# Opening of a fused cross-attention and routed-FFN kernel: scales in four chains, small loads on ScalarE's queue, weights in pieces

## The reference, cut to what matters

```python
x  = x + tanh(g_xattn) * xattn(ctx_1024, layernorm(x), ln_m_g, ln_m_b, ln_l_g, ln_l_b, Wq, Wkv, Wout)
x  = x + tanh(g_ffn)   * ffn(layernorm(x), gate_w, w1, b1, w2, b2)

def xattn(ctx, latents, ...):          # 32 batches, 375 context rows, 112 latents, width 256, 16 heads of 64
    c   = layer_norm(ctx) * ln_m_g + ln_m_b
    lat = layer_norm(latents) * ln_l_g + ln_l_b
    q   = lat @ Wq                                  # [256, 1024]
    k, v = split(concat([c, lat]) @ Wkv)            # [256, 2048]; 487 rows
    return (softmax(q @ k.T / 8) @ v) @ Wout        # [1024, 256]
# ffn: softmax gate over 8 experts, top 2, exact gelu, hidden width 1024
```

## Time and profile before

| | |
|---|---|
| median of 3 timed runs | 1902.32 us (1900.02 to 1903.77) |
| the profiled execution's own time | 1902.62 us |
| its span | 1900.9 us |
| mean granted TensorE clock, of full | 0.951 |
| busy: PE, PEld | 1674.2 us (88%), 1163.1 us (61%) |
| busy: DVE, ACT, POOL | 1428.0 us (75%), 1195.3 us (63%), 1183.0 us (62%) |
| HBM read, written | 78.66 MB, 20.19 MB |

### The profile page before, as it was taken

One profiled execution on the slowest core, in us unless ns is written; L12 is line 12 of the kernel. 1 busy time (PEld: TensorE's weight loads), 2 busy tenths in 40 slices (PEclk: granted clock), 3 DMA queues, 4 the chain that ended last, 5 costly groups with the idle time before them and its releaser, 6 DMA issues. The chain is left out here.

```text
span 1900.9 us, 42714 instructions
## 1 busy us (share of the span) xinstructions
PE 1674.2 (88%) x15031; PEld 1163.1 (61%) x15032; DVE 1428.0 (75%) x2917; ACT 1195.3 (63%) x2666; POOL 1183.0 (62%) x1297
## 2 busy tenths in 40 slices
PE   2899999999999999999999999998402999999980
PEld 1456666666666666666666666665302999989970
DVE  4777888888888888888888888877395666666646
ACT  2587777777777777877777777777254333433320
POOL 4477777777777777777777777767263343333320
PEclk9999999999999999999999999999555999999995
DMA  3267766767767666676776776767455111111119
GB/s 131 46 127 140 142 144 131 139 139 142 147 129 145 138 140 144 135 139 138 139 150 136 136 137 129 138 130 142 118 186 173 46 49 45 50 50 47 47 35 289
DMA packets 599541, 233.18 MB, mean 123 GB/s; under 512 B 534064, under 2 KB 584016, under 8 KB 598992
## 3 DMA queue, kind: packets, MB, share of 16 engines
q1 hardware_dynamic: 592656, 212.67, 52.5%
q0 software_dynamic: 6720, 18.36, 3.1%
HBM read 78.66 MB, written 20.19 MB: 52 GB/s over the span
## 5 line engine op out<-in xcount | busy, mean ns | idle before, releaser
L279 POOL TENSOR_TENSOR p_parts<-p_f,p_parts 112x487 f16<-112x487 f32 x512 | 560.4, 1118 | 194.2 <-ACT p_parts L374 194.2
L365 ACT ACTIVATE p_f<-scores_ps,shift 112x487 f32<-112x487 f32 x512 | 337.0, 663 | 13.3 <-DVE shift L500 9.7
L495 DVE TENSOR_REDUCE neg_max<-scores_ps 112x1 f32<-112x487 f32 x512 | 313.0, 654 | 27.1 <-PE scores_ps L653 27.1
L402 ACT ACTIVATE k_hi<-proj_ps 128x488 fp32r<-128x488 f32 x256 | 147.9, 578 | 262.5 <-PE proj_ps L635 262.5
L1018 ACT ACTIVATE space<-h_ps,b_sb,undo 128x256 f32<-128x256 f32 x280 | 142.8, 560 | 232.1 <-PE h_ps L1247 228.8
L374 ACT ACTIVATE p_parts<-p_f 112x487 f16<-112x487 f32 x512 | 275.9, 607 | 0.0
L536 DVE SCALAR_TENSOR_TENSOR v_sb<-proj_ps,v_sb 128x512 f16<-128x512 f32 (+1 forms) x256 | 176.5, 689 | 92.1 <-ACT v_sb L416 89.4
L530 DVE TENSOR_TENSOR k_lo<-proj_ps,k_hi 128x488 fp32r<-128x488 f32 x256 | 168.2, 657 | 78.2 <-ACT k_hi L402 78.0
L684 PE MATMUL pv_ps<-v_sb,pt_sb 128*128 128x128 f16 x2048 | 218.9, 221 | 7.8 <-DMA pt_sb<-p_parts 7.8
L635 PE MATMUL proj_ps<-kv_hi,wkv_hi 128*128 128x488 f16 x512 | 192.3, 376 | 22.0 <-POOL kv_lo L306 13.5
L635 PE MATMUL proj_ps<-wkv_hi,kv_hi 128*128 128x512 f16 (+1 forms) x512 | 194.6, 380 | 0.1
(11 more groups left out here) (222 smaller groups left out, 4075.1 us busy)
## 6 DMA issues: line engine op xcount, KB each, us to landing
w_part<-in_L_ffn_w_dram SPq DMA_DIRECT2D x64, 256.0 KB, 3.5
stage<-in_L_ffn_w_dram SPq DMA_DIRECT2D x32, 512.0 KB, 4.1
ctx_sb<-in_ctx_dram SPq DMA_DIRECT2D x32, 375.0 KB
space<-y_rows SPq DMA_DIRECT2D x32, 224.0 KB, 4.7
pt_sb<-p_parts SPq DMA_TRANSPOSE x256, 4.0
x_sb<-in_x_dram SPq DMA_DIRECT2D x32, 112.0 KB
res_sb<-in_x_dram SPq DMA_DIRECT2D x32, 112.0 KB, 5.3
x_dram<-x_sb SPq DMA_DIRECT2D x32, 112.0 KB, 2.9
```

The lines of the kernel that those rows point to most:

```text
L279: pool.tensor_tensor(p_parts[0:LQ, p % PS, h, 1, 0:LK], p_f[0:LQ, p % 2, h, 0:LK], p_parts[0:LQ, p % PS, h, 0, 0:LK], ALU.subtract).then_i ...
L365: act.activation(p_f[0:LQ, p % 2, h, 0:LK], scores_ps[n][0:LQ, 0:LK], ACT.Exp, bias=shift[0:LQ, p // 2 % 2, n:n + 1], accum_out=row_sum[0: ...
L402: act.activation(k_hi[:, j], ps[:, 0:LKP], ACT.Copy).then_inc(kq_high, 1)
L495: dve.tensor_reduce(neg_max[0:LQ, p // 2 % 2, n:n + 1], scores_ps[n][0:LQ, 0:LK], AX.X, ALU.max, negate=True).then_inc(max_done, 1)
```

## The change

- The six small loads are issued from ScalarE's queue, ahead of its tanh. The four layer-norm vectors count on `small_loaded`, the other two on semaphores of their own.
- wkv is loaded in four pieces of 512 columns (rows of 2 KB), in the order keys 0 to 3, values half 0, keys 4 to 7, values half 1, each with a semaphore of its own; wq and wout follow as before, then batch 1.
- The five peaks go through four separate chains ("turns"), each with TensorE's transpose and spread: the layer-norm vectors (0), wkv (1), wq (2), wout (3). Turns 0 and 1 run before the loop on TensorE and at t = -22 on VectorE; turns 2 and 3 are spread over t = -11 to -2. The small peaks are taken at t = -24, ahead of batch 0's statistics.
- The high and low parts of wkv are made by pieces: `kv0` and `kv1` (ScalarE t = -14, VectorE t = -11), `kv2` (t = -8, -7), `kv3` (t = -6, -5); wq by halves `q0` (t = -6, -5) and `q1` (t = -4, -3); wout whole (t = -1, 0). TensorE waits for `kv1` at its first projection, `kv3` at j = 4, `q0` and `q1` at their query projections.
- The staging places of wkv and wout move to `p_parts` and `pt_sb`; the padding of `p_parts` is cleared by GpSimd at t = -1 and ScalarE waits for it at t = 0; the padding of `pt_sb` is cleared at t = 1 behind the low part of wout, for which SyncE waits ahead of its first transpose. The first clearing in `v_sb` moves ahead of GpSimd's loop.

```diff
@@ sync
-            for k in range(KD):
-                sp.dma_start(stage[:, k], wkv[k * 128:(k + 1) * 128]).then_inc(w_loaded, 16)
-            for n, a in enumerate((ln_m_g, ln_m_b, ln_l_g, ln_l_b)):
-                sp.dma_start(affine[:, n, :], a.rearrange("(k p) -> p k", p=128), allow_slow_non_contiguous=True).then_inc(small_loaded, 16)
-            sp.dma_start(tanh_g[:, :], g_x.partition_broadcast(128)).then_inc(small_loaded, 16)
-            sp.dma_start(gate_sb[:, :, :], gate_w.rearrange("(k p) e -> p k e", p=128)).then_inc(small_loaded, 16)
+            for n in range(4):
+                sp.dma_start(kv_chunk(stage, n), kv_chunk(wkv.rearrange("(k p) n -> p k n", p=128), n)).then_inc(w_loaded[n], 16)
...
+                    if p == 0:
+                        sp.wait_ge(w_ready, W_TURN["out"])
@@ gpsimd
-            for s in range(PS):
-                pool.memset(p_parts[0:LQ, s, :, :, LK:512], 0.0).then_inc(pool_step, 1)
-            pool.memset(pt_sb[:, :, 16 * LQ:], 0.0).then_inc(pool_step, 1)
...
+            pool.memset(v_sb[96:128, 0, KT - 1], 0.0).then_inc(v_cleared, 1)
...
                 if t == -1:
-                    pool.wait_ge(w_ready, 4)
+                    pool.wait_ge(w_ready, W_TURN["q1"])
                     pool.wait_ge(kvlo_done, 4)
                     pool.wait_ge(pool_step, subtracted(2))
+                    for s in range(PS):
+                        pool.memset(p_parts[0:LQ, s, :, :, LK:512], 0.0).then_inc(parts_cleared, 1)
...
+                if t == 1:
+                    pool.wait_ge(w_ready, W_TURN["out"])
+                    pool.memset(pt_sb[:, :, 16 * LQ:], 0.0).then_inc(parts_cleared, 1)
@@ scalar
-            act.wait_ge(small_loaded, 16 * 6)
+            for n, a in enumerate((ln_m_g, ln_m_b, ln_l_g, ln_l_b)):
+                act.dma_start(affine[:, n, :], a.rearrange("(k p) -> p k", p=128), allow_slow_non_contiguous=True).then_inc(small_loaded, 16)
+            act.dma_start(tanh_g[:, :], g_x.partition_broadcast(128)).then_inc(tanh_loaded, 16)
+            act.dma_start(gate_sb[:, :, :], gate_w.rearrange("(k p) e -> p k e", p=128)).then_inc(gate_loaded, 16)
+            act.wait_ge(tanh_loaded, 16)
             act.activation(tanh_g[:, :], tanh_g[:, :], ACT.Tanh).then_inc(tanh_done, 1)
...
+                if t == -2 * NP + 2:
+                    weight_high("kv0")
+                    weight_high("kv1")
                 if t == 0:
-                    act.wait_ge(set_up, 2)
+                    act.wait_ge(parts_cleared, PS)
...
+                for turn, at in (("kv2", -8), ("q0", -6), ("kv3", -6), ("q1", -4), ("out", -1)):
+                    if t == at:
+                        weight_high(turn)
@@ vector
+            def largest(turn, first, last):
+                at = slice(first, last)
+                dve.wait_ge(peaks_moved, 4 * turn + 2)
+                then(dve.tensor_reduce(peak_t[0:last - first, :], tail_ps[0:last - first, 0:128], AX.X, ALU.max))
+                then(dve.tensor_scalar(peak_diag[0:last - first, at], ident[0:last - first, 0:last - first], peak_t[0:last - first, :], None, ALU.mult))
+                dve.sem_inc(peaks_moved, 1)
+            def power(turn, first, last):
+                at = slice(first, last)
+                dve.wait_ge(peaks_moved, 4 * turn + 4)
+                then(dve.tensor_copy(peak_e[:, at], tail_ps[:, 128:128 + last - first]))
...
+            def kv_scale():
+                for n in range(4):
+                    dve.wait_ge(w_loaded[n], 16)
+                    last = dve.tensor_reduce(peak_kv[:, n:n + 1], kv_chunk(stage, n), AX.XY, ALU.max, apply_absolute_value=True)
+                then(last)
+                then(dve.tensor_reduce(peak[:, 0:1], peak_kv[:, :], AX.X, ALU.max))
+                dve.sem_inc(peaks_moved, 1)
+                largest(1, 0, 1)
+                power(1, 0, 1)
+                dve.sem_inc(scales_ready, 1)
+            def q_peak():
+                dve.wait_ge(wq_loaded, 16)
+                then(dve.tensor_reduce(peak[:, 1:2], stage_q, AX.XY, ALU.max, apply_absolute_value=True))
+                dve.sem_inc(peaks_moved, 1)
+            def q_scale():
+                power(2, 1, 2)
+                then(dve.tensor_tensor(undo[:, 2:3], inverse[:, 3:4], inverse[:, 0:1], ALU.mult))
+                then(dve.tensor_scalar(undo[:, 4:5], undo[:, 2:3], inverse[:, 3:4], float(DH) ** -0.5, ALU.mult, ALU.mult))
+                then(dve.tensor_scalar(undo[:, 0:1], undo[:, 4:5], inverse[:, 1:2], None, ALU.mult))
+                dve.sem_inc(scales_ready, 1)
...
+                if t == -3 * NP:
+                    input_peaks()
                 if t == -3 * NP + 2:
-                    weight_scales()
+                    input_scale()
+                    kv_scale()
                 if t == -NP - 3:
-                    split_kv_weights()
-                if t == -NP + 2:
-                    split_q_weights()
-                if t == -2:
-                    split_out_weights()
+                    weight_low("kv0")
+                    weight_low("kv1")
+                    q_peak()
...
+                for turn, at in (("kv2", -7), ("q0", -5), ("kv3", -5), ("q1", -3), ("out", 0)):
+                    if t == at:
+                        weight_low(turn)
+                if t == -8:
+                    largest(2, 1, 2)
+                if t == -6:
+                    q_scale()
+                if t == -4:
+                    out_peak()
+                if t == -3:
+                    largest(3, 2, 3)
+                if t == -2:
+                    out_scale()
@@ tensor
+            for turn, first, last in ((0, 3, 5), (1, 0, 1)):
+                turn_peaks(turn, first, last)
+                spread_peaks(turn, first, last)
...
                         if b == -1:
-                            pe.wait_ge(w_ready, 2)
+                            pe.wait_ge(w_ready, W_TURN["kv1"])
+                    if b == -1 and j == 4:
+                        pe.wait_ge(w_ready, W_TURN["kv3"])
...
+                if t == -8:
+                    turn_peaks(2, 1, 2)
+                if t == -7:
+                    spread_peaks(2, 1, 2)
+                if t == -3:
+                    turn_peaks(3, 2, 3)
+                if t == -2:
+                    spread_peaks(3, 2, 3)
```

More of the change, by code:

```diff
@@ L85, in attention @@
         peak = sb("att_peak", [128, 5])
+        peak_kv = sb("att_peak_kv", [128, 4])
         peak_t = sb("att_peak_t", [5, 1])
@@ new lines, in input_peaks, with input_scale @@
+            def input_peaks():
+                dve.wait_ge(small_loaded, 16 * 4)
+                dve.tensor_reduce(peak[:, 3:4], affine[:, 0:4:2, :], AX.XY, ALU.max, apply_absolute_value=True)
+                then(dve.tensor_reduce(peak[:, 4:5], affine[:, 1:4:2, :], AX.XY, ALU.max, apply_absolute_value=True))
+                dve.sem_inc(peaks_moved, 1)
+            def input_scale():
+                largest(0, 3, 5)
+                power(0, 3, 5)
+                then(dve.tensor_scalar(affine[:, :, :].rearrange("p a k -> p (a k)"), affine[:, :, :].rearrange("p a k -> p (a k)"), scale[:, 3:4], None, ALU.mult))
@@ L611, in _, with turn_peaks, spread_peaks @@
             pe.wait_ge(set_up, 1)
[L612 to L615 removed]
+            def turn_peaks(turn, first, last):
+                pe.wait_ge(peaks_moved, 4 * turn + 1)
+                nc.tensor.transpose(tail_ps[0:last - first, 0:128], peak[:, first:last], ident[:, :]).then_inc(peaks_moved, 1)
+            def spread_peaks(turn, first, last):
+                pe.wait_ge(peaks_moved, 4 * turn + 3)
+                nc.tensor.matmul(tail_ps[:, 128:128 + last - first], ones[0:last - first, :], peak_diag[0:last - first, first:last],
+                                 start=True, stop=True).then_inc(peaks_moved, 1)
+            for turn, first, last in ((0, 3, 5), (1, 0, 1)):
+                turn_peaks(turn, first, last)
+                spread_peaks(turn, first, last)
             def take(kind, index):
```

116 lines of the change are left out of this document (58 added, 58 removed).

## The result

| | before | after |
|---|---|---|
| timed runs, median us | 1902.11 (5) | 1912.42 (5) |
| ratio, 95% interval | | 1.0053 (1.0039 to 1.0068) |
| profiled execution: time, span | 1902.62, 1900.9 | 1912.42, 1910.6 |
| first small peak on VectorE | 14.27 | 12.32 |
| statistics of batch 1 | 28.19 | 26.35 |

The kernel is slower by half a per cent. The first projection does start earlier, by 4.0 us, but the first scores come 5.5 us later and those of step 4 7.5 us later. From there the distance stays: 7.5 us again at the start of the FFN part. The remaining 2.2 us of the 9.7 between the spans arise in the FFN part, whose code is the same in both. In the fourteen kernels profiled here that part took from 536.2 to 541.2 us, in no order that follows the opening, so nothing is built on it.

What follows compares the result with a forecast made beforehand. TensorE's own work bounds the steady part, so an earlier opening moves the end one for one. Opening -9.3, eight steps +7.7 and step 0 +1.6 sum to 0.0: 1902.3 us, range 1896.5 to 1907.

Steps and rivals of the forecast that it cites:

- L: Opening: time at which the four layer-norm vector loads have landed; taken as 8.0 us, bounds 6 to 11.5.
- The prediction's other estimate: Opening: small loads landing at about 6.5 us if DMA engines go round their queues packet by packet; total unchanged.
- the small loads come late: Rival, VectorE's first wait: landing at 11.5 us makes the kernel slower, +3.9, 1906.2 us; chance 0.20.
- The scale chain behind L: Opening, after the small loads land: peaks, batch 0's statistics and two scale chains up to wkv's scales, 12.9 us.
- The load of batch 1 as the wait that replaces the chain: Opening: batch 1 lands at 21.0 us, so its statistics start at 21.2 instead of 28.19, a gain of 7.0.
- From batch 1's statistics to P: Opening, up to TensorE's first projection (P): 9.85 us instead of 12.16, with P at 31.05, a gain of 9.3.
- The eight steps: From first projection towards first scores: the moved scale and low-half work returns, +7.7 us, bounds 4 to 8.5.
- Step 0: First attention step: wout's low half on VectorE, 2.25 us net less 0.62 of slack, delays the next maxima by +1.6.
- the one in which the opening's gain comes through: Rival: eight steps grow by only 4 us and step 0 by nothing, -5.3, or 1897.0 us; chance 0.25.
- a P later than 34 us: Sign of being wrong: TensorE's first projection (P), forecast at about 31 us, comes later than 34.
- the chunk peaks did not wait for wkv: Sign of being wrong, opening: chunk peaks waiting for wkv data would make supply, not the chain, the bound.
- The net of zero: Whole kernel: opening -9.3, eight steps +7.7, step 0 +1.6, sum 0.0; work moved, not removed; chance 0.55.

Runs made afterwards that it cites:

- b3: Changed kernel with the four layer-norm vectors loaded as eight 512-byte rows, turned by TensorE, tanh_g and gate issued once they have landed; 1907.92 us.
- a2: Changed kernel with the two peaks of the small loads taken behind batch 0's statistics and moments; 1907.33 us.
- c2: Kernel before, with layer-norm vectors as rows, batch 1 loaded ahead of wq and wout, short wkv chain, whole weights, 12 unread matmuls; median 1897.84 us, ratio 0.9977.
- c3: Changed kernel with the layer-norm vectors as eight 512-byte rows and wkv loaded in two halves of 8 KB rows; 1908.11 us.
- d1: Changed kernel with layer-norm vectors as eight rows, wkv in two 8 KB-row halves, and unread matmuls in three TensorE holes; median 1905.69 us, ratio 1.0018.
- b1: Changed kernel with unread matmuls filling three TensorE holes (steps -5, -3 and 2); first projection to first scores 40.5 us instead of 42.3, total not given.
- a3: Changed kernel without wout's low half at step 0 (zeros instead); scores of steps 0 and 4 17.25 us apart instead of 19.17, total not given.
- c1: Kernel before with only the transfers changed: small loads on ScalarE's queue, wkv in four pieces, single scale chain and whole weights kept; 1903.21 us.
- a1: Changed kernel with the six small loads put back on SyncE's queue behind wkv's four pieces; 1911.27 us.

## Why the prediction was wrong

The forecast was 1902.3, within 0.2% of no change, and the kernel is slower by 0.53%, outside the range of 1896.5 to 1907. Its steps, with the 7.45 us by which step 4's scores miss it:

1. *L, the landing of the small loads: 8.0 forecast, 12.2 measured. This is the largest error, +3.9* (4.2 less the 0.3 by which the load of batch 1 was to hide it). The bounds of 6 to 11.5 came from the same kind of load behind wkv and with nothing ahead. Neither row has two queues at work, and no count of rows was made: 1024 rows of 4 bytes against 2 KB packets. b3 shows it: with eight rows in their place the vectors had landed by 7.3. The rival "the small loads come late" named the right place, and its upper end was too low. The prediction's other estimate, 6.5 by the rule of the Trainium skill, was farther off still.
2. *The scale chain behind L: 12.9 forecast, 14.15 measured (12.2 to 26.35), +1.25.* Two instructions, L488 and L499, took 1.64 us instead of 0.40. Durations were copied from the old chain, which ran while GpSimd was idle. Now batch 0's statistics are late, and GpSimd's normalisation falls beside the chain: L488 ends at 17.92 where GpSimd's L331 ends at 17.90, and L499 at 18.50 where L332 ends at 18.48. The same pattern stands in a2 (L481, 14.71 + 1.19, against L314, 14.42 + 1.47) and in c2 (L457, 30.20 + 1.12, against GpSimd's kv_lo, 30.20 + 1.10). It was read from timelines; no run took it away alone.
3. *The load of batch 1 as the wait that replaces the chain:* not reached, since the chain was later. In b3, where it was reached, it was at 24.2, not 21.0: the gap that the forecast saw close did close (366 GB/s from 11 to 13 us, against 15), but wkv's smaller rows took 0.8 to 1.1 us (c3, d1); the rest of the 3 us is open.
4. *From batch 1's statistics to P:* 9.85 forecast, 10.03 measured. The shortened kv_lo was right (3.39), and so was the free place for wq's peak.
5. *The eight steps: +7.7 forecast, +9.45 measured.* The path was right: first query projection released at P + 21.1 forecast, 20.6 measured; key projection of step -4 at 22.5 and 21.8; the longest hole for wq's low half. From there the error is +1.7: key projection of step -1 at 35.35 and 37.0, query low at 41.4 and 43.2. It is the granted clock, a term that the forecast had at nothing; b1 takes it away and leaves 7.65. That this meets the 7.7 so closely is in part luck: d1 leaves 6.7, and the slow start alone differs by up to 1 us between runs. In the details the walk was less good: it had one wait of over 4 us for the low half of wq, and there were two, of 2.95 us for that and of 1.98 for the affine behind the peak of wout.
6. *Step 0: +1.6 forecast, +1.97 measured;* a3 gives 1.9. The 0.62 of slack did not help.

Sum of errors: 3.9 + 1.25 + 0.2 + 1.75 + 0.35 = 7.45. Of the 9.7 between the spans the other 2.2 lie in the FFN part, and are open; the medians are 10.3 apart, as the profiled run of the kernel before was 0.5 above its median. Of the rivals, the one in which the opening's gain comes through fell: TensorE's busy time between 80 and 120 us fell from 36.00 to 33.80, instead of filling up. (Part of that is that the stretch now begins 5.5 us earlier in the work.) Of the prediction's own signs of being wrong one came, a P later than 34 us; the chunk peaks did not wait for wkv. The main idea held, that the change moves work out of a preparation where it was cheap into steps where TensorE waits for VectorE (c1, d1). The net of zero did not: L and the chain were sized by rows in which the competing queue or engine was idle, and the clock had no term.

## What to carry to other kernels

Count rows as well as bytes: here small loads of 1024 rows of 4 bytes, beside a large one on another queue, moved at about one row for each packet of the large one, and slowed it too. As a few long rows they landed 4 to 5 us earlier. Work taken off a serial opening is only gained if it lands where an engine is idle; put in the order of use, between producer and consumer, it is paid again, and the hole it leaves before TensorE can cost its clock besides, in one execution more than in another. Copy a duration from a trace only with what the neighbouring engines did at the time.

## What the runs showed that was not expected

- The granted clock fell behind single holes of 2 to 3 us: in the changed kernel after 1.98 us of idle, with another hole of 2.95 us ended 7 us before it, and some 6 us ran at 1.2 GHz. All three holes filled gave back 1.8 us (b1 against the changed kernel) or 3.5 (d1 against c3). The same hole of 2.95 us was followed by a fall in a3, b3 and c3 and by none in the changed kernel, a1 and a2.
- About a one-for-one turn of two DMA queues, with 4-byte packets against 2 KB ones (647 and 600 packets in 4 us, 285 GB/s instead of the 333 and 353 of a1 and b3).
- VectorE's small instructions took 1.10 and 1.19 us instead of 0.17 and 0.16, each ending together with a GpSimd instruction (L488 and L331 in the changed kernel, L481 and L314 in a2). The Trainium skill (SBUF — State Buffer, "Who interferes with whom") describes such exclusion for vector instructions with two inputs in SBUF and for those that take both ports; the rows here agree: L481 has two inputs, and of the chain's one-input instructions in the changed kernel those on one element a partition kept their 0.15 us beside a running GpSimd, and the one on two elements waited. Not every row does: in the changed kernel L481 took its 0.16 us at 15.88 beside a GpSimd instruction of 1.06 us that had started at 15.29.
